# Maxima of two attention stages led by 24 chunks instead of 28, their transposition one step later, and bulk transfers moved behind the row transfers

## The reference, cut to what matters

```python
x = x + attn_a(layernorm(x), ...)      # 32 heads of width 8, softmax over 1024 keys, biases
x = x + ffn(layernorm(x), ...)         # silu(x wg) * (x wu), 2:4 sparsified, times w_down
x = x + attn_b(layernorm(x), ...)      # 32 query heads, 8 key/value heads, a band of 128 keys masked
x = x + ffn(layernorm(x), ...)
# both attentions: softmax(q k^T * scale) v, for 2 batches of 1024 tokens, hidden size 256
```

## Time and profile before

| what | value |
|---|---|
| median of 3 runs | 1703.85 us (1703.78 to 1711.48) |
| the profiled execution: own time, span | 1705.32 us, 1703.5 us |
| mean granted TensorE clock | 0.988 |
| busy PE, DVE, ACT, POOL | 97%, 86%, 75%, 16% of the span |

### The profile page before, as it was taken

How to read it: one execution, slowest core, us unless ns; L and a number is a source line. 1 busy time by engine, 2 the same in 40 slices (tenths; PEclk the granted TensorE clock), 3 DMA queues, 4 the chain that set the end, 5 groups by cost and what they waited for, 6 DMA issues and landing times.

```text
span 1703.5 us, 38923 instructions
## 1 busy us (share of the span) xinstructions
PE 1653.8 (97%) x13872; PEld 654.6 (38%) x13872; DVE 1471.7 (86%) x2144; ACT 1281.6 (75%) x2424; POOL 266.7 (16%) x623
## 2 busy tenths in 40 slices
PE   7899999999999999999988999999999999999999
PEld 4322222222222224776653222222222222247777
DVE  6999999999999992665678999999999999837655
ACT  3299999999999997333224999999999999963220
POOL 1410000000000000000012223333223333310000
PEclk9989999999999999999997999999999999999999
DMA  6964433345333312100405222233222222211000
GB/s 166 293 152 85 75 61 68 61 84 86 69 64 67 61 33 73 53 1 1 114 14 147 53 50 56 50 65 75 50 53 56 53 56 63 57 39 38 13 13 25
DMA packets 72126, 114.68 MB, mean 67 GB/s; under 512 B 12464, under 2 KB 27824, under 8 KB 71984
## 3 DMA queue, kind: packets, MB, share of 16 engines
q1 hardware_dynamic: 71984, 112.63, 29.2%
HBM read 71.96 MB, written 40.63 MB: 66 GB/s over the span
## 4 chain that ended last, share of the span: by engine, by line
PE 88%; DVE 4%; DMA 4%; ACT 1%; issue 1%; SPq 0%; POOLq 0%; ACTq 0%; DVEq 0%
PE psum L742 32%; PE psum L724 20%; PE psum L800 13%; PE psum L694 12%; PE psum L822 6%; DMA max_rows<-mT 2%; PE psum L657 2%; DVE mneg L1214 2%; PE psum L780 2%; PE psum L677 1%; DMA area<-max_rows 1%; PE psum L639 1%; ACT area L988 1%; PE psum L712 1%; DVE xn L1220 1%
## 5 line engine op out<-in xcount | busy, mean ns | idle before, releaser
L988 ACT ACTIVATE area<-psum 128x512 f32<-128x512 f32 x2048 | 1097.9, 601 | 45.1 <-PE psum L724 17.9
L742 PE MATMUL psum<-area 128*32 128x256 f32 x8192 | 655.7, 393 | 0.6 <-POOL area L1471 0.4
L724 PE MATMUL psum<-area 51*128 51x512 bf16 x2048 | 640.3, 386 | 4.6 <-DMA area<-max_rows 3.6
L1220 DVE CUSTOM_DVE_ANT_0 xn<-psum,band 128x1024 f32<-128x1024 f32 x512 | 588.4, 1233 | 11.7 <-PE psum L694 11.2
L1214 DVE TENSOR_REDUCE mneg<-psum 128x1 f32<-128x1024 f32 x512 | 582.0, 1215 | 9.2 <-PE psum L694 8.8
L742 PEld LDWEIGHTS psum<-area 128*32 128x32 f32 x8192 | 162.3, 108 | 401.0 <-issue 263.2
L694 PE MATMUL psum<-area 48*128 48x512 bf16 x1024 | 301.8, 386 | 10.7 <-DVE mneg L1214 7.7
L724 PEld LDWEIGHTS psum<-area 51*128 51x128 bf16 x2048 | 143.1, 94 | 428.2 <-ACT area L988 353.3
L694 PE MATMUL psum<-k_max_b,area 48*128 48x512 bf16 x1024 | 291.9, 387 | 8.7 <-DVE mneg L1220 7.9
L1031 ACT ACTIVATE area<-psum 128x512 f32<-128x512 f32 x64 | 38.2, 597 | 161.5 <-PE psum L800 161.5
L1452 POOL TENSOR_TENSOR mparts<-mneg,nought 128x16 bf16<-128x16 f32 x64 | 14.1, 220 | 719.0 <-DVE mneg L1214 505.3
(11 more groups left out here) (74 smaller groups left out, 831.0 us busy)
## 6 DMA issues: line engine op xcount, KB each, us to landing
ctx_rows<-area SPq DMA_DIRECT2D x64, 256.0 KB, 3.5
area<-q_stacks SPq DMA_DIRECT2D x32, 384.0 KB, 7.1
area<-k_stacks SPq DMA_DIRECT2D x64, 192.0 KB, 5.7
area<-q_stacks_b SPq DMA_DIRECT2D x32, 384.0 KB, 5.8
area<-q_stacks SPq DMA_DIRECT2D x32, 192.0 KB, 4.3
area<-q_stacks_b SPq DMA_DIRECT2D x32, 192.0 KB, 3.4
area<-ctx_rows SPq DMA_DIRECT2D x16, 256.0 KB, 4.7
area<-inv_rows SPq DMA_DIRECT2D x16, 256.0 KB, 5.4
```

The source lines that it names most:

```text
L724: pe.matmul(psum[:, BANK_OF["exp", g, u, head], :], k_st[lo:lo + ROWS + PARTS, buf, 0 if a else head // 2, kt * P:(kt + 1) * P], q_st[lo:l ...
L742: mm = pe.matmul(psum[head * VW:(head + 1) * VW, BANK_OF["ctx", g, qh], cols], vaug[:, buf, kt, head, :], probs[:, u % PRING, head, cols], ...
L988: act.activation(probs[:, u % PRING, head, :], psum[:, BANK_OF["exp", like, u, head], :], ACT.Exp, scale=SCALE).then_inc(bank_freed, 1)
L1220: dve.tensor_tensor_reduce(band_out[:, c % 2, :], slot, band[:, at:at + SEQ], 1.0, -3.0e38, ALU.add, ALU.max, mneg[:, qh, col:col + 1]).th ...
```

## The change

Chunks lead by 24 (SHIFT 4) instead of 28. The split on POOL thus moves from units 2 and 10 to 4 and 12, and the transposition on PE from units 4 and 12 to 5 and 13 (TURN 5). The projected tiles of the last group move from units 8 to 11 to units 10 to 13. On SP each group's load of the stack for the maxima goes behind the first row transfer, two of the four early stores behind the first row transfer of all, and the weights to later places. The reciprocals of batch 0's sums go from the middle of the groups to behind the last maximum, and so do the store and the load of the inverses. The copies of V on DVE come one chunk earlier.

```diff
-SHIFT = 2
-TURN = 4
+TILE_AT = 10
+SHIFT = 4
+TURN = 5
 LEAD = CHUNKS - 2 * SHIFT
...
-        V_CHUNKS = [(1, 5, CPH + 1, CPH + 3, CPH + 5, CPH + 7), (CPH + 3, CPH + 5, CPH + 7, CPH + 8)]
+        V_CHUNKS = [(1, 5, CPH + 1, CPH + 3, CPH + 5, CPH + 7), (CPH + 3, CPH + 5, CPH + 6, CPH + 7)]
...
-            def group(a, g, buf, first=False, ahead=2, inverses=None):
+            def group(a, g, buf, first=False, ahead=2):
                 if ahead >= 1:
                     load_st_stack(a, g + 1, 1 - buf)
-                if ahead >= 2:
-                    load_max_stack(a, g + 2, buf)
+                else:
+                    store_inverses(a, 0)
                 if not first:
                     store_ctx(a, g - 1, 1)
                 move_max(a, g, buf, 1)
-                if first and a == 0:
-                    load_late_weights()
+                if ahead == 2:
+                    load_max_stack(a, g + 2, buf)
+                elif ahead == 1:
+                    sp.wait_ge(max_ready, CHUNKS * (GROUPS * a + g + 1))
+                    for c in range(HALF):
+                        load_ctx(a, c)
+                else:
+                    sp.wait_ge(max_ready, CHUNKS * GROUPS * (a + 1))
+                    sp.wait_ge(inv_stored, 16 * (BATCH * a + 1))
+                    for c in range(HALF):
+                        load_inv(a, c)
                 store_ctx(a, g, 0)
...
             for a in range(2):
                 if a == 0:
                     store_first_stacks()
-                store_stacks(a, 0)
+                    store_stacks(0, 0, range(2, 4))
+                else:
+                    store_stacks(1, 0, range(3))
...
-                store_stacks(a, 1)
-                if a == 0:
-                    move_max(a, 0, 0, 0)
+                if a == 0:
+                    store_stacks(0, 1, range(2))
+                    move_max(0, 0, 0, 0)
+                    store_stacks(0, 1, range(2, 4))
+                else:
+                    store_stacks(1, 1, range(3))
                 group(a, 0, 0, first=True)
+                if a == 0:
+                    load_weights_b()
...
-                group(a, GPB + 2, 0, inverses=0)
+                group(a, GPB + 2, 0)
+                if a == 0:
+                    load_dense_weights()
...
-                sp.wait_ge(max_ready, CHUNKS * GROUPS * (a + 1))
-                load_ctx(a, 0)
                 group(a, GROUPS - 1, 1, ahead=0)
...
-                    if not ahead and BT <= u < BT + CT:
-                        project_tile(a, u - BT)
+                    if not ahead and TILE_AT <= u < TILE_AT + CT:
+                        project_tile(a, u - TILE_AT)
...
+                    if first and a == 0 and 1 <= u <= 2:
+                        stacks_out(0, (u + 1,))
                     if first and a == 1 and u == BT:
-                        stacks_out(a)
+                        stacks_out(1, range(3))
...
                 if a == 0:
                     copy_turned(a, 0, 0, 0)
-                    stacks_out(a)
+                    stacks_out(0, range(2))
...
-                    if a and c - 1 == V_CHUNKS[a][-1]:
+                    if a and c == V_CHUNKS[a][-1]:
                         copy_v(a, 1, 0)
-                    if a == 0 and c - 1 in V_CHUNKS[a]:
-                        copy_v(a, *divmod(V_EARLY + V_CHUNKS[a].index(c - 1), VCH[0]))
+                    if a == 0 and c in V_CHUNKS[a]:
+                        copy_v(a, *divmod(V_EARLY + V_CHUNKS[a].index(c), VCH[0]))
...
-                group(a, GPB + 1)
-                invert_sums(a, 0)
-                group(a, GPB + 2)
-                with dve.Fori(GPB // 2 + 1, (GROUPS - 2) // 2) as i:
+                with dve.Fori(GPB // 2, (GROUPS - 2) // 2) as i:
                     group(a, 2 * i + 1)
                     group(a, 2 * i + 2)
+                invert_sums(a, 0)
                 divide_ctx(a, 0)
                 divide_ctx(a, 1)
```

More of the change, by code:

```diff
@@ L407, in _, with load_weights_b, load_dense_weights @@
                 sp.dma_start(w[:], src.rearrange("(k p) n -> p k n", p=P)).then_inc(w_loaded[0], 16)
-            def load_late_weights():
+            def load_weights_b():
                 for w, src in zip((*wqo_b, *wkv_b), (wq_b, wo_b, wk_b, wv_b)):
                     sp.dma_start(w[:], src.rearrange("(k p) n -> p k n", p=P)).then_inc(w_loaded[1], 16)
+            def load_dense_weights():
                 for w, src in ((wg, w_gate), (wu, w_up)):
@@ L438, in split_whole, with store_stacks @@
                 sp.wait_ge(lo_done, PBASE[a] + b * PCH[a] + ORDER[a].index((j, 1)) + 1)
-            def store_stacks(a, b):
-                for j, (w, m, rows) in enumerate(QUARTERS[a]):
+            def store_stacks(a, b, quarters):
+                for j in quarters:
+                    w, m, rows = QUARTERS[a][j]
                     n = QBASE[a] + b * NQ[a] + j
-                    if a == 0 and b == 0 and j < 2:
-                        continue
                     split_whole(a, b, j)
@@ L539, in group @@
                     move_max(a, g + 1, 1 - buf, 0)
-                if inverses is not None:
-                    store_inverses(a, inverses)
             def stored_all(a, batches):
@@ L611, in _ @@
                 store_inverses(a, 1)
-                load_ctx(a, 1)
+                sp.wait_ge(inv_stored, 16 * BATCH * (a + 1))
+                for c in (HALF, HALF + 1):
+                    sp.wait_ge(o_ready, 8 * a + 2 * (c - 1))
+                    load_ctx(a, c)
+                    load_inv(a, c)
             for c in range(TILES // 2):
@@ L1039, in silu_and_size, with stacks_out @@
                                        ACT.Abs).then_inc(mag_done, 1)
-            def stacks_out(a):
+            def stacks_out(a, quarters):
                 n = QBASE[a] + BATCH * NQ[a]
-                for i in sorted(set(SLOT[n - NQ[a]:n])):
+                for i in sorted(SLOT[n - NQ[a] + j] for j in quarters):
                     act.wait_ge(stacks_stored[i], stored(i, n))
```

31 lines of the change are left out of this document (15 added, 16 removed).

## The result

The changed kernel takes **1713.1 us** (median of 14 runs, 1711.6 to 1721.0) against 1704.3 us before on the same chips. The ratio is 1.0049, with a 95% interval of 1.0034 to 1.0065: slower, by just about the 0.5% that can be told from no change. Forecast were 1696.4 us, faster than before, and a range of 1692 to 1702.

A forecast was written before the change was run, and what follows sets the result against it. DVE was taken to pace the groups, PE having little to spare. Terms of -5.4 us in attention 0 and -2.0 in attention 1, together -7.4, gave 1697.9 against the profiled execution, 1696.4 as median; range 1692 to 1702.

The forecast's parts named there:

- the one on the turn: From a half's last chunk to its transposition: three steps suffice; free in attention 0, +2.1 us in attention 1.
- PE's reserve: PE's spare time against DVE's pace: 0.02 us a step in attention 0, 0.034 in attention 1 (0.30 a half).
- the 3.23: Microseconds from PE's start on a half's last chunk until its split parts reach PE; claimed to fit three steps, 3.33.
- My rival for this term: "The turn is not regained": the turn costs 11.8 us instead of 2.1, time 1706; chance 0.06.
- Opening of attention 0: Before group 0: earlier rows let it start at 80.1 us instead of 84.21, behind the last V copy; -4.1 us.
- the clock's rival: Group 0's start: a shorter hole leaves PE at 2.4 GHz, each opening gives 2 us more, 1692.4; chance 0.10.
- Opening of attention 1: Before group 0: the last copy of V ends at 919.8 us instead of 920.99; -1.2 us.
- Reciprocals and late rows: Inside the groups: reciprocals moved behind the last maximum, -3.4 us; DVE's waits for reciprocal and late rows gone, -1.6.
- Last group: Attentions 0 and 1: rows +0.2, -0.9; turn +0.1, +0.4; tile at unit 10 +0.2 each; added chunk units +0.3 each.
- Rows after the turn: Three units, 6.8 us, for rows needing 5.9 behind the transposition; cover 0.9 us, cost nothing.
- The rival had the mechanism at 1733: Rows too late: transfers delayed 1.5 us beyond the cover in half of the 62 halves, 1733 us; chance 0.05.
- the last group is late: Last group: inverses and rows queue on SP behind the reciprocal, both waits 1.5 us more per attention, 1701.5; chance 0.12.

The follow-up runs named there:

- run 1: Changed kernel with the old lead and old turn (SHIFT 2, TURN 4, LEAD 28), everything else of the change kept: 1699.7 us.
- run 2: Changed kernel with SHIFT 3 alone changed (LEAD 26, TURN stays 5): 1692.9 us.
- run 3: Changed kernel with POOL's last two split operations left out, the third part of the maxima zero (less exact scores): 1695.3 us.
- run 6: Changed kernel with SHIFT 3 and TURN 4 (LEAD 26, three steps between a half's last chunk and its transposition): 1726.8 us.
- run 11: Changed kernel with LEAD 26 and POOL's split made longer, its fourth operation done ten times: 1755.5 us.
- run 12: Changed kernel with the masking of the probabilities in attention 1 left out: 1711.4 us.
- run 9: Kernel before, with only each attention's first reciprocal moved behind the last maximum, plus the dependent stores, loads and tiles: 1704.2 us.
- run 7: Changed kernel with TURN 6 (LEAD 24, five steps to the transposition, two units for the rows): 1730.4 us.
- run 4: Kernel before, with only the change's lead and turn (SHIFT 4, TURN 5) and V copies one chunk earlier; transfers, reciprocals and tiles as before: 1833.0 us.
- run 8: Changed kernel (LEAD 24) with the transposition issued behind the chunk's matmul of its step instead of ahead of the step: 1709.7 us.

## Why the prediction was wrong, step by step

**The step that failed** is the one on the turn: "If PE is further ahead, it waits until it is not, and DVE loses nothing", and "PE regains ... and waits it off again". It looked at the distance from PE's chunk to PE's transposition. It didn't ask what DVE does while PE waits. DVE has at most two chunks lying ready behind the half's last one, and the third stands on PE behind the transposition. So the path is a loop over DVE, and PE's reserve doesn't enter it: time that the pacing engine stands still is regained by nobody. Runs 1, 2, 3, 6 and 11 show it from four sides: the chunks in the loop, its length down, its length up, and its independence of the lead.

Two sizes went with it. From the chunk's start on PE to DVE's start I took 0.43 us from the opening; inside the groups it is 0.64 (258.61 to 259.25), in attention 1 0.82. And the transposition's own 0.17 us ahead of that chunk was not in the 3.23. With both the sum is 3.61 us in attention 0, which set against DVE's 3.39 says 0.2 us a half. But right sizes alone would not have saved the forecast: by my rule, PE's wait less PE's reserve, the waits as measured (0.28 and 0.37 us) cost 0.2 us a half in attention 0 and 0.07 in attention 1, and measured are 0.27 and 0.43.

**What it cost.** Attention 0: 0.27 us in each of 30 halves, 8.1 us, forecast 0. Attention 1: 0.43, 12.9 us, forecast 2.1. Together some 21 us in place of 2.1. The size of PE's own wait, 0.38 us, was forecast nearly right for attention 1 (0.37) but for a wrong reason: I put it down to unit 3's masking, and run 12 refutes that. My rival for this term had 11.8 us as its upper bound. It was too small because it held attention 0 to be free, and because DVE's loss is larger than PE's wait.

**The signs.** I had named three by which the prediction would be wrong. Halves of 18.5 us or more came in attention 1 (18.74), not in attention 0 (18.36). ACT waiting for stores in group 0 came once, 1.12 us at 86.28 us in attention 0, within the 1.5 that I allowed. The tile at unit 10 waits only 0.1 us. PE's waits of 0.1 to 0.4 us, which I took for a sign of being right, came too: they don't tell a free turn from a costly one.

**The rest of the sum held.** Without its 2.1 us for the turn the forecast is 1694.3 us. Run 3, in which the loop fits and the rest of the change stands, measured 1695.3, and run 2, with two chunks more of lead, 1692.9. In detail:

- *Opening of attention 0*: first score at 79.37, forecast 80.1, gated by the last copy of V as said: -4.8 us. Counted from the opening's transposition it is -4.1 (8.25 us instead of 12.38), as forecast; the other 0.7 lie ahead of it. Behind the first score another 0.7 us were gained, with a clock at full rate from 88.9 us on instead of 95.2. That looks like the clock's rival at a third of its size, but in runs 3 and 12, whose opening is the same, this gain is missing (14.7 and 15.0 us from the first score to the next transposition against 13.9 here and 14.6 before, counted to the same unit). So it belongs to this execution and not to the change.
- *Opening of attention 1*: first score 16.85 us behind the opening's transposition instead of 17.78, -0.9, forecast -1.2. On the way to the first turn inside the group it lost 1.1 again, for which I had nothing: the slow phase began later and lasted as long (clock 0.50 until about 935 us, 931 before). These two are not settled either: in run 3 the same opening took 15.3 us to the first score and lost 0.1 behind it.
- *Reciprocals and late rows*: forecast -3.4 and -1.6. In run 9 the halves gain 4.6 us, as forecast for the two reciprocals and the wait behind the second (1.7 + 1.7 + 1.2); the time gained 3.6. The late rows of attention 0 were undersized: four long halves hold 1.7 us, not 0.4.
- *Last group*: from the last transposition to ACT's next table load +0.1 us in attention 0 and -0.6 in attention 1, one unit of 2.24 taken off; forecast +0.8 and 0.0. The tile at unit 10 waits 0.1 us for DVE.
- *Rows after the turn*, costed at nothing: right, but only through the moved loads. The cover is real (run 7 takes it away and is 37 us slower than run 2), and what would have happened without the move is run 4: 1833 us. The rival had the mechanism at 1733; it took 1.5 us beyond the cover where PE waited 3.8 on average in attention 0, and it left out the clock.
- *A sum that doesn't come out*: the rival "the last group is late" says 1701.5. Two waits of 1.5 us more in each of two attentions are 6 us, which is 1702.4. Nothing rests on it.
- *ACT's reserve*: the 0.9 us a half that I gave it were not tested. Run 8 looked like a test, but there PE is the bound.

## What to carry to other kernels

When a result of the pacing engine comes back to it by way of others, write the path as a loop that starts and ends on that engine, and compare it with the work which is already lying ready for it. What exceeds that is lost in every round, and the reserve of the others doesn't help. Before a distance is shortened, look for the wall on both sides: here the loop on one side (three chunks are too few), the rows on the other (two units are too few). Of the placements tried, LEAD 26 with the turn at unit 5 has room on both sides and was the fastest, 12 us faster than before; the old lead with the old turn has room too, but a longer opening (run 1).

Price a transfer on the critical path by what is issued ahead of it in its queue, and a hole in PE by the slow steps behind it. When an engine waits a little more and the time goes up, look at the steps of each engine in one round before naming the bound: in run 8 the engine with the new wait was not the one that set the pace.

## What was not expected of the hardware

- With four loads and a context store ahead of it on the same queue, a 12 KB transfer held up the next issue for 6.1 to 8.6 us, against 1.4 to 2.8 with these loads behind it (attention 0, run 4 and the changed kernel).
- In the hole of 5.28 us PE's clock fell to half, and PE ran at half rate for the next 5.5 us. At such holes in attention 0 of run 4 the loss was about one and a half times the wait. Shorter holes can do it too: in run 7 a half with a wait of 1.85 us lost 4.6 us.
- A matmul issued between two that run side by side costs more than its own time: the transposition costs a step of PE 0.23 us ahead of it (1.34 against 1.11), and 0.48 in the middle of it (run 8).
- A busy share counts overlapping instructions from start to end. ACT is busy for 98% inside the groups of attention 0 of the kernel before (17.74 of 18.09 us), and yet its exponentials, 0.59 us long, follow each other at 0.48 where nothing holds them (run 8, 240.68 to 241.65), against 0.55 on average there.
